# Last stage of a transformer layer: ScalarE writes the normalised rows, one DMA queue carries loads and stores

## The reference

```
x = layernorm(x + attention(x))      # 16 heads of 16, softmax over 512 keys, projection and bias
x = layernorm(x + moe_ffn(x))        # 8 experts of hidden width 512, the 2 best experts of each row
layernorm(x) = (x - mean) / sqrt(var + 1e-5)   # over the 256 numbers of a row, no gain, no bias
```

## Time and profile before

| | us |
|---|---|
| Median of 3 runs | 3741.0 |
| Lowest and highest run | 3740.78 and 3743.41 |
| Span of the profiled execution, first to last instruction | 3738.5 |
| `final_norm` in that span: from its first load at 3636.0 to the end | 102.5 |

### The profile page before, as it was taken

How to read it: one execution, slowest core, us unless ns; L and a number is a source line. 1 busy time by engine, 2 the same in 40 slices (tenths; PEclk the granted TensorE clock), 3 DMA queues, 4 the chain that set the end, 5 groups by cost and what they waited for, 6 DMA issues and landing times. The chain is left out here.

```text
span 3738.5 us, 68180 instructions
## 1 busy us (share of the span) xinstructions
PE 3498.9 (94%) x19714; PEld 2455.3 (66%) x19714; DVE 2507.9 (67%) x5866; ACT 2007.2 (54%) x3877; POOL 1171.2 (31%) x929
## 2 busy tenths in 40 slices
PE   5999999999999999999999968999999999999970
PEld 3555565555555555555556537888888888888860
DVE  6787787777778778778777745455555545454539
ACT  2666666666666666666666653444444444444420
POOL 3013213122131231221312233343444535353334
PEclk8999999999999999999999989999999999999985
DMA  6777777756565555555555624444434443443439
GB/s 114 153 156 158 167 151 172 128 92 106 87 107 93 93 105 88 95 104 92 106 91 91 105 71 78 62 75 69 63 64 63 74 64 62 60 68 50 57 56 337
DMA packets 410259, 376.39 MB, mean 101 GB/s; under 512 B 249528, under 2 KB 311360, under 8 KB 409920
## 3 DMA queue, kind: packets, MB, share of 16 engines
q1 hardware_dynamic: 346944, 287.82, 41.5%
q0 software_dynamic: 58368, 67.74, 11.5%
q10 hardware_dynamic: 4608, 16.78, 1.1%
HBM read 89.92 MB, written 152.17 MB: 65 GB/s over the span
## 5 line engine op out<-in xcount | busy, mean ns | idle before, releaser
L880 DVE TENSOR_REDUCE peak<-ps_rows 128x1 f32<-128x512 f32 x2048 | 1349.7, 681 | 477.8 <-PE ps_rows L557 460.9
L648 ACT ACTIVATE probs<-ps_cols 128x512 f32<-128x512 f32 x2048 | 1120.5, 600 | 378.5 <-PE ps_cols L566 375.2
L557 PE MATMUL ps_rows<-stack 128*128 128x512 f32 x2048 | 893.8, 438 | 46.5 <-issue 33.3
L1088 PE MATMUL ps_hid<-x_hi,stack 128*128 128x512 f32 x2560 | 804.6, 395 | 33.0 <-DVE x_lo L1181 28.4
L566 PE MATMUL ps_cols<-stack 128*128 128x512 f32 x2048 | 813.1, 398 | 2.3 <-ACT probs L648 1.9
L1058 POOL DMA_INDIRECT x<-out,token x320 | 503.6, 1574 | 797.7 <-ACT out L1144 657.6
L1187 DVE TENSOR_TENSOR hid<-ps_hid,act_in 128x512 f32<-128x512 f32 x320 | 218.8, 688 | 599.0 <-ACT act_in L1130 598.8
L557 PEld LDWEIGHTS ps_rows<-stack 128*128 128x128 f32 x2048 | 389.6, 190 | 309.7 <-DVE peak L880 213.5
L1088 PEld LDWEIGHTS ps_hid<-x_hi,stack 128*128 128x128 f32 x2560 | 476.6, 189 | 142.5 <-DVE x_lo L1181 28.5
L579 PE MATMUL ps_pv<-probs,v 128*17 128x512 f32 x4096 | 545.1, 604 | 0.9 <-ACT probs L648 0.9
L423 POOL TENSOR_SCALAR var_eps<-mv 128x4 f32<-128x4 f32 x32 | 7.5, 234 | 1593.9 <-DVE mv L752 1593.9
(11 more groups left out here) (130 smaller groups left out, 3575.5 us busy)
## 6 DMA issues: line engine op xcount, KB each, us to landing
stack<-qk_hi SPq DMA_DIRECT2D x512, 128.0 KB
stack<-qk_lo SPq DMA_DIRECT2D x512, 128.0 KB
expert_rows<-blank SPq DMA_DIRECT2D x80, 520.0 KB, 5.0
quarters<-expert_rows SPq DMA_DIRECT2D x320, 128.0 KB, 2.7
xs<-in_L_attn_x SPq DMA_DIRECT2D x32, 512.0 KB, 3.4
x<-row SPq DMA_DIRECT2D x32, 512.0 KB
fy<-x SPq DMA_DIRECT2D x32, 512.0 KB, 4.7
out<-fz ACTq DMA_DIRECT2D x32, 512.0 KB, 4.9
```

Of the source, the lines that this page charges most:

```text
L557: pe.matmul(ps_rows[n % ROWS][:], q_stack[s][:, h, t * P:(t + 1) * P], k_stack[s][:, h, :], start=True, stop=True).then_inc(s_rows, 1)
L648: act.activation(probs[:, j % RING, :], ps_cols[j % 2][:], ACT.Exp, scale=SCALE).then_inc(s_exp, 1)
L880: dve.tensor_reduce(peak[s % 2][:, j:j + 1], ps_rows[n % ROWS][:], AX.X, ALU.max, negate=True).then_inc(s_max, 1)
L1088: last = pe.matmul(ps_hid[f % 2][:, part, :], w[c.par][:, k, cols], xx[c.odd][:, k, :], start=i == 0, stop=i == 3 * KT - 1)
```

## The change

The normalising moves from VectorE to ScalarE. With rstd and shift = -mean * rstd, the row is rstd * y + shift, which ScalarE's activation instruction computes with a scale and a bias for each partition. VectorE keeps the statistics and gets one small instruction for each chunk that computes `shift` for its four rows a partition. ScalarE no longer issues stores; SyncE issues both, the store of chunk i-3 behind the load of chunk i. GpSimd's instructions are the same.

```
+        shift = [sb(f"fshift{i}", [P, TILES]) for i in range(RING_Y)]
...
         @block.sync
         def _(sp):
+            def store(i, r):
+                sp.wait_ge(s_norm, i * TILES + TILES)
+                settle(sp, s_waited_sp)
+                sp.dma_start(out_rows[i], z[r][:].rearrange("p t c -> p (t c)")).then_inc(s_store[r], 16)
+
             def body(i, r, q):
                 wait(sp, s_norm, i * TILES - (RING_Y - 1) * TILES)
                 if not isinstance(i, int):
                     settle(sp, s_waited_sp)
                 sp.dma_start(y[r][:].rearrange("p t c -> p (t c)"), y_rows[i]).then_inc(s_in[r], 16)
+                if not isinstance(i, int) or i >= RING_Y - 1:
+                    store(i - (RING_Y - 1), (r + 1) % RING_Y)
 
             rings(sp, body)
+            for i in range(n_chunks - (RING_Y - 1), n_chunks):
+                store(i, i % RING_Y)
+            for r in range(RING_Y):
+                sp.wait_ge(s_store[r], 16 * (n_chunks // RING_Y))
 
         @block.scalar
         def _(act):
             def body(i, r, q):
-                act.wait_ge(s_norm, i * TILES + TILES)
-                settle(act, s_waited_act)
-                act.dma_start(out_rows[i], z[r][:].rearrange("p t c -> p (t c)")).then_inc(s_store[r], 16)
+                act.wait_ge(s_shift, i + 1)
+                wait(act, s_store[r], q * 16)
+                for t in range(TILES):
+                    act.activation(z[r][:, t, :], y[r][:, t, :], ACT.Identity, bias=shift[r][:, t:t + 1],
+                                   scale=rstd[r][:, t:t + 1]).then_inc(s_norm, 1)
...
         @block.vector
-            def normalise(i, r, q):
+            def shifts(i, r):
                 dve.wait_ge(s_rstd, i + 1)
-                wait(dve, s_store[r], q * 16)
-                for t in range(TILES):
-                    dve.tensor_scalar(z[r][:, t, :], y[r][:, t, :], mv[r][:, t, 0:1], rstd[r][:, t:t + 1],
-                                      ALU.subtract, ALU.mult).then_inc(s_norm, 1)
+                wait(dve, s_norm, i * TILES - (RING_Y - 1) * TILES)
+                dve.scalar_tensor_tensor(shift[r][:], mv[r][:, :, 0], -1.0, rstd[r][:],
+                                         ALU.mult, ALU.mult).then_inc(s_shift, 1)
...
             def body(i, r, q):
                 statistics(i, r, q)
+                if not isinstance(i, int) or i:
+                    shifts(i - 1, (r - 1) % RING_Y)
```

More of the change, by code:

```diff
@@ L1255, in final_norm @@
         s_rstd = sem("s_frstd")
+        s_shift = sem("s_fshift")
         s_norm = sem("s_fnorm")
-        s_waited_sp, s_waited_act = sem("s_waited_sp_f"), sem("s_waited_act_f")
+        s_waited_sp = sem("s_waited_sp_f")
         s_waited_pool, s_waited_dve = sem("s_waited_pool_f"), sem("s_waited_dve_f")
@@ L1284, in body @@
             def body(i, r, q):
-                act.wait_ge(s_norm, i * TILES + TILES)
-                settle(act, s_waited_act)
-                act.dma_start(out_rows[i], z[r][:].rearrange("p t c -> p (t c)")).then_inc(s_store[r], 16)
+                act.wait_ge(s_shift, i + 1)
[3 more added lines that the diff above has]
+                                   scale=rstd[r][:, t:t + 1]).then_inc(s_norm, 1)
             rings(act, body)
-            for r in range(RING_Y):
-                act.wait_ge(s_store[r], 16 * (n_chunks // RING_Y))
         @block.gpsimd
@@ L1317, in statistics @@
                     dve.bn_aggr(mv[r][:, t, :], stats[r][:, t, :]).then_inc(s_bn, 1)
-            def normalise(i, r, q):
+            def shifts(i, r):
                 dve.wait_ge(s_rstd, i + 1)
-                wait(dve, s_store[r], q * 16)
-                for t in range(TILES):
-                    dve.tensor_scalar(z[r][:, t, :], y[r][:, t, :], mv[r][:, t, 0:1], rstd[r][:, t:t + 1],
-                                      ALU.subtract, ALU.mult).then_inc(s_norm, 1)
+                wait(dve, s_norm, i * TILES - (RING_Y - 1) * TILES)
+                dve.scalar_tensor_tensor(shift[r][:], mv[r][:, :, 0], -1.0, rstd[r][:],
+                                         ALU.mult, ALU.mult).then_inc(s_shift, 1)
             def body(i, r, q):
                 statistics(i, r, q)
[L1329 to L1335, removed]
+                if not isinstance(i, int) or i:
+                    shifts(i - 1, (r - 1) % RING_Y)
             rings(dve, body)
-            normalise(n_chunks - 1, RING_Y - 1, n_chunks // RING_Y - 1)
+            shifts(n_chunks - 1, RING_Y - 1)
 def transformer_layer(nc, x, w_qkv, w_proj, b_proj, w_gate, w1, w2, out):
```

## The result

The changed kernel is slower. Over 20 runs of each its median is 3751.49 us (3748.25 to 3756.97) against 3742.65 us (3738.21 to 3748.44) of the kernel before on the same chip: a ratio of 1.0025, interval 1.0018 to 1.0031. The forecast was 3741.0 us with a range up to 3748, so the time lies 3.5 us above the range and on the side to which 0.09 had been given. The kernel before had been at 3741.0 us in its first 3 runs and is at 3742.65 us over 20; set against that, the forecast was no change and the change is 8.8 us.

A forecast was written before the change was run, and what follows sets the result against it. VectorE was taken to bound the last stage at 2.965 us a chunk; a circle of 4.7 + 4.06 = 8.76 us, 2.92 a chunk, gives back 1.4 us, beginning and end cost 1.0 and 0.4: 3741.0 us, range 3734 to 3748.

The forecast's parts named there:

- What bounded the kernel before: Last stage, 102.5 us: VectorE sets the pace at 2.965 us a chunk; the DMA engines carry what it asks.
- The circle: Last stage: buffer reuse from normalising through load and statistics to normalising three chunks on, 8.76 us, 2.92 a chunk.
- From landed to normalised: Circle's compute part: statistics 1.68, shift 0.17, handovers 0.12, ScalarE's block 2.09, together 4.06 us.
- L: Circle's other part, from a chunk normalised to its buffer's next load landed: 4.7 us, between 4.35 and 4.92.
- the pair: One load and one store, 0.524 MB each; the load's last byte was still to be the pair's last.
- the slow first microsecond of a pair: Possible gain at the start of load and store together: L might be 4.57 or even 4.35 us.
- Rival 2: Last stage: DMA engines already at their limit with mixed reads and writes, pace stays 2.965, 3742.4 us; chance 0.14.
- Rival 3: Last stage: one queue serialises, load waits for store, L 6.12, circle 10.18, 14.2 us more, 3755; chance 0.09.
- Rival 1: Last stage: shorter circle, DMA engines' own rate bounds at 2.56 us a chunk, 11.8 us less, 3729; chance 0.07.
- Rival 4: ScalarE must load a table for the new function, a single 1.3 us or so at the start; given nothing.
- Beginning and end: Last stage: chunk 0 normalised 1.0 us later, chunk 31 2.09 us after chunk 30; they cost 1.0 and 0.4.

The follow-up runs named there:

- The queue part alone: Kernel before with SyncE issuing loads and stores, ScalarE without work, VectorE normalising as before: last stage 106.5 us, 3923.1 us, ratio 1.0007.
- The quarter stores: Changed kernel, four buffers, each store writing only the first quarter of its chunk: last stage 99.1 us, 2.85 us a chunk.
- the two queues: Changed kernel with ScalarE issuing stores behind its own activations and SyncE only loads, four buffers: last stage 107.5 us, 3925.22 us, ratio 1.0014.

## Why the prediction was wrong, point by point

**What bounded the kernel before: right.** VectorE, 2.965 us a chunk, with no help from more buffers.

**The circle as the new bound: right.** Eight buffers take it away, the shift on GpSimd makes it span four chunks, less work for ScalarE shortens it, and each change moves the pace by about the circle's sum, taken with the landing that the run itself shows.

**From landed to normalised: right.** 4.06 us was predicted. Chunk 30's statistics begin at 3735.68, when its load has landed, and the block of chunk 29 that waits for them ends at 3737.56 + 2.07 = 3739.63: 3.95.

```profile
3735.68 1.41 DVE L1326 BATCH_NORM_STATS2 fstats<-fy 128x6 f32<-128x256 f32 x4 [1.23 <-DMA fy<-x]
...
3737.56 2.07 ACT L1301 ACTIVATE fz<-fy,fshift,frstd 128x256 f32<-128x256 f32 x4 [0.92 <-DVE fshift L1335]
```

An activation with scale and bias was put at 605 ns and is 588 in the mean; the block was put at 2.09 us and is 2.07. The shift was put at 0.17 and is 0.16.

**L, from normalised to landed: the step that failed.** The prediction took 4.7, between 4.35 and 4.92, with the words that the later issue "costs nothing as long as the load used to land only when nearly all of the pair had been moved". Measured, ten circles run from the end of chunk 0 (3642.84 + 2.07 = 3644.9) to the end of chunk 30 (3743.1): 9.82 us each, so L is 9.82 - 3.95 = 5.87. That is 1.17 too little, ten times: 11.7 us, of which the 0.11 too much in the other part gives 1.1 back. That makes 10.6 us; chunk 0 was 0.5 us earlier than forecast, so chunk 30 was 10.1 us late, and chunk 31 in fact 10.0.

The 5.87 has two parts. The issue comes 0.93 us after the normalising; 0.72 had been counted and then held to be free. And the load lands 4.8 to 5.0 us after its own issue, where the 4.7 would have allowed 4.0. The thought behind it was that the pair's bytes are the same in any order, so that a load issued later would land so much sooner after its issue. It did not. The queue part alone shows this with VectorE's block in place: issue 0.93, landing 5.0. The quarter stores show that the store ahead is in it: the landing falls to 3.5. The semaphore events of the trace show the order: the store of chunk 7, issued at 3667.14, lands at 3671.31, and the load of chunk 11, issued at 3667.84, lands at 3672.65, 1.34 us behind it, where 0.524 MB at 410 GB/s are 1.28 us. Putting the load in front (5.4) only puts it behind the store of the chunk before. So in this one queue the load came behind the store issued before it: in all 28 such pairs of the changed kernel it landed after that store, 1.20 us later at least and 1.68 in the median. Whether it would wait as long for a store in another queue is not shown: the 5.0 of the two queues was measured on another chip than the 4.7, and the kernel before has 5.0 on such a chip too. The gain that I had hoped for, the slow first microsecond of a pair, did not come: in slices of 1.5 us from 3660 to 3720 us the rate of the changed kernel goes up and down between 197 and 407 GB/s, and that of the kernel before between 262 and 415. One such fall in the changed kernel (columns as before):

```profile
3667.00:3669.00 2.00, 0.00 (x0) 0.00 (x0) 1.15 (x8) 0.74 (x2) 0.61 (x2) 0.50 1.01 389
3669.25:3670.75 1.50, 0.00 (x0) 0.00 (x0) 1.28 (x4) 1.08 (x3) 0.39 (x1) 0.50 0.88 238
3670.75:3672.50 1.75, 0.00 (x0) 0.00 (x0) 0.57 (x6) 1.15 (x3) 0.94 (x2) 0.50 0.97 382
```

**The rivals.** Rival 2, a limit near 353 GB/s for mixed traffic, falls with the 418 GB/s of eight buffers. Rival 3 named the place, the load behind the store, and the point from which it decides, L above 5.45. Its price of 14.2 us was for a complete serialisation (6.12); the truth is 5.87, between it and the forecast and nearer to it. The sign that the prediction gave for it, a wait of 1.5 us or more for each load, is what came: 43.0 / 28 = 1.54. It was given a chance of 0.09. Rival 1, the DMA engines' own rate, is what eight buffers reach: 2.51 us a chunk at 418 GB/s, where it had 2.56 at 410. Rival 4 did not come: in the last stage of the changed kernel ScalarE has its 128 activations and no table load. The two table loads of the span, in the stages before it, took 1283 ns each.

**Beginning and end: nearly right.** Chunk 0 was to be normalised 1.0 us later in the span and was 0.5, since the stage began 0.4 earlier; chunk 31 follows chunk 30 by 1.97 instead of 2.09.

## What to carry to other kernels

When work leaves the engine that was the bound, write down the circle through the buffers before counting any gain: issue lag, landing, every block between landing and release, divided by the chunks it spans. Count the issue lag in full, and do not let the landing shrink by it: here a load issued 0.7 us later behind a store landed no sooner after its issue (5.0 us, before 4.7). And since the circle is run through ten times, a term that is 1.2 us too small costs 12 us. The cure here was buffers and not engines: the same change with eight instead of four turns 0.25% slower into 0.42% faster than the kernel before (0.9958, interval 0.9945 to 0.9971, and again 0.9959), while the kernel before gains nothing from them (a last stage of 102.6 us, before 102.5).

## What the runs showed of the hardware

- A DMA share of 1.01 was no limit reached here. The share was 1.01 at 354 GB/s in the kernel before (3680 to 3700 us), 0.92 at 311 in the changed one (the same stretch), and 1.03 at 418 with eight buffers (3840 to 3860 us). In the trace's records of single packets of 4 KB the median lasts 159 ns in all three. In the kernel before, chunks 8 to 27, 272 of the 640 packets that are among the first 32 of a load's 128 last over 300 ns, up to 1025, and only 114 of the other 1920. The mean of the load queue was 214 ns before the change and that of the one mixed queue 192 after it (3660 to 3720 us); stores of the kernel before have a mean of 159. With eight buffers and a backlog the mean of the one mixed queue is 159. That the slow packets are a load's start without anything ahead of it to cover it fits these runs; no run isolates it, and that part stays open.
- Loads and stores mixed reached 418 GB/s in one queue and 417 in two, both with eight buffers. With four buffers the issuing time lay in the circle: SyncE's issue of the store, 0.35 us, and the register work behind it put the load 0.7 us later (3667.14 to 3667.84).
- ScalarE's activation from SBUF to SBUF of 128x256 with scale and bias for each partition took 588 ns, and four in a row 2.07 us.
